# Top-10 cross-attention: reordered input loads and softmax steps in the first two batches

## The reference, cut to what matters

```python
scores = einsum('bnd,d->bn', x, score_w[0]) + score_b[0]      # x: (8, 224, 512)
_, topk_idx = top_k(scores, 10)
sparse = take_along_axis(x, topk_idx)                          # (8, 10, 512)
q = (sparse @ Wq.T + bq), split into 16 heads of 32
k = (ctx @ Wk.T + bk); v = (ctx @ Wv.T + bv)                   # ctx: (8, 750, 512)
attn = softmax(q @ k.T / sqrt(32))
out = x.at[arange(8), topk_idx].set((attn @ v) @ out_w.T + out_b)
```

## Time and profile before

| | |
|---|---|
| median of 3 runs | 141.36 us (141.33 to 141.48) |
| the profiled execution | time 141.29 us, span 139.5 us |
| granted TensorE clock, mean | 0.995 of full speed |
| busy: TensorE, VectorE, ScalarE, GpSimd | 95%, 63%, 18%, 5% |
| moved by DMA | 37.52 MB, mean 269 GB/s |

### The profile page before, as it was taken

The page is one execution under the profiler, slowest core; times in us unless marked ns, Lnnn a source line. Parts: engine busy times, 40 slices in busy tenths (PEclk is TensorE's granted clock), DMA queues, the critical chain, the costliest instruction groups (busy, mean ns, idle before and its releaser), DMA issues.

```text
span 139.5 us, 3090 instructions
## 1 busy us (share of the span) xinstructions
PE 132.1 (95%) x1298; PEld 126.2 (90%) x1298; DVE 88.5 (63%) x247; ACT 24.9 (18%) x53; POOL 7.5 (5%) x34
## 2 busy tenths in 40 slices
PE   4989999899999999999999999999999999999980
PEld 2567999789999999999999999999999999999970
DVE  1798696899890577287870575077218799874150
ACT  4122400030322160003140031004101400231110
POOL 7700000003000000000000000000000000000002
PEclk9999999999999999999999999999999999999998
DMA  4999999999997189999989985996691092000001
GB/s 131 415 414 417 409 411 401 444 434 413 416 385 308 46 332 401 271 401 435 427 328 314 318 343 147 318 324 266 222 316 45 5 331 120 0 0 5 0 5 47
DMA packets 6958, 37.52 MB, mean 269 GB/s; under 512 B 961, under 2 KB 961, under 8 KB 4642
## 3 DMA queue, kind: packets, MB, share of 16 engines
q1 hardware_dynamic: 6528, 37.00, 69.7%
q0 software_dynamic: 128, 0.33, 0.7%
q10 hardware_dynamic: 290, 0.01, 0.2%
HBM read 33.50 MB, written 3.83 MB: 268 GB/s over the span
## 4 chain that ended last, share of the span: by engine, by line
PE 72%; DMA 14%; SPq 7%; issue 2%; DVE 1%; POOLq 1%; POOL 0%; DVEq 0%
PE mix_ps L846 38%; PE logits_ps L827 23%; DMA ctx_r<-ctx_rows_dram 14%; PE logits_ps L813 5%; SPq L205 3%; SPq L212 3%; PE logits_ps L785 2%; PE logits_ps L751 1%; PE mix_ps L785 1%; POOLq L60 1%; DVE o_T L610 1%; PE misc_ps L859 1%; DVE heads L607 1%; PE logits_ps L859 0%; SPq L218 0%
## 5 line engine op out<-in xcount | busy, mean ns | idle before, releaser
L846 PE MATMUL mix_ps<-probs,ctx_r 125*128 125x160 f32 x384 | 54.0, 300 | 0.3
L846 PEld LDWEIGHTS mix_ps<-probs,ctx_r 125*128 125x128 f32 x384 | 52.5, 190 | 0.8 <-DMA ctx_r<-ctx_rows_dram 0.4
L827 PE MATMUL logits_ps<-qk,ctx_c 128*125 128x160 f32 x240 | 33.4, 299 | 0.0
L827 PEld LDWEIGHTS logits_ps<-qk,ctx_c 128*125 128x125 f32 x240 | 32.9, 188 | 0.0
L813 PE MATMUL logits_ps<-qk,ctx_c 128*125 128x160 f32 x144 | 20.6, 302 | 0.7 <-DMA ctx_c<-ctx_cols_dram 0.7
L533 DVE TENSOR_REDUCE col_max<-logits_ps 125x160 f32<-125x960 f32 x8 | 9.3, 1157 | 18.8 <-PE logits_ps L827 15.2
L813 PEld LDWEIGHTS logits_ps<-qk,ctx_c 128*125 128x125 f32 x144 | 19.7, 187 | 1.1 <-DMA ctx_c<-ctx_cols_dram 0.9
L361 ACT ACTIVATE mix<-mix_ps 128x320 f32<-128x320 f32 x16 | 7.0, 439 | 62.1 <-PE mix_ps L846 62.1
L572 DVE TENSOR_REDUCE prob_sum<-probs 125x160 f32<-125x960 f32 x8 | 14.7, 1842 | 4.4 <-ACT probs L357 4.4
L357 ACT ACTIVATE probs<-probs 125x480 f32<-125x480 f32 x16 | 9.3, 603 | 30.3 <-DVE probs L565 30.3
L408 DVE CUSTOM_DVE_ANT_0 product<-x_sb,score_w_sb 112x513 f32<-112x513 f32 x16 | 10.4, 692 | 1.3 <-DMA x_sb<-x_lines_dram 1.2
(11 more groups left out here) (130 smaller groups left out, 96.1 us busy)
## 6 DMA issues: line engine op xcount, KB each, us to landing
ctx_r<-ctx_rows_dram SPq DMA_DIRECT2D x8, 1536.0 KB, 8.0
ctx_c<-ctx_cols_dram SPq DMA_DIRECT2D x6, 1500.0 KB, 10.8
x_sb<-x_lines_dram SPq DMA_DIRECT2D x8, 520.0 KB, 9.5
out_dram<-x_sb SPq DMA_DIRECT2D x8, 448.0 KB, 12.8
ctx_c<-ctx_cols_dram SPq DMA_DIRECT2D x2, 750.0 KB, 14.5
ctx_c<-ctx_cols_dram SPq DMA_DIRECT2D x4, 375.0 KB, 15.5
wq_sb<-wq_dram SPq DMA_DIRECT2D x1, 1024.0 KB, 7.5
wk_sb<-wk_dram SPq DMA_DIRECT2D x1, 1024.0 KB, 10.0
```

The lines of the kernel that those rows point to most:

```text
L827: last = nc.tensor.matmul(logits_ps[n][0:S_P, t // BANK_T, (t % BANK_T) * HQ:(t % BANK_T + 1) * HQ], ctx_c[n][:, f, t, :], qk[:, b, f, :], ...
L846: last = nc.tensor.matmul(mix_ps[half][:, f * HQ:(f + 1) * HQ], ctx_r[n][0:S_P, t, c:c + P], probs[n][:, t, :], start=(t == 0), stop=(t == ...
```

## The change

- SP: the score weights are issued first on SP's queue and no longer by ScalarE. Among the first loads, the columns' parts move ahead of inputs: part 0 of batch 0 ahead of input 4, part 1 ahead of input 5, the first two parts of batch 1 ahead of input 6, the third ahead of input 7. Rows 0 are loaded in two parts, each with its own semaphore (`part_rows_in`).
- SP waits for `gathered` ahead of columns 3.
- VectorE: the maximum is taken in two halves, by PSUM banks, each behind its own semaphore (`first_logits`, `logits_done`), and find_shift's reductions take both halves. score(7) moves behind subtract_max(0, 0). The softmax steps of batch 1 move between choose_eight and choose_rest.
- TensorE: weigh(0) becomes `weigh_by_part`, which does context groups 0 to 2 of all four feature tiles first and 3 to 5 after. transpose_scores moves from matmul 8 to 22 of logits(1), transpose_picked from 14 to 15 and project_queries(1) from 19 to 20 of weigh(1).

```diff
+ROW_PARTS = [(0, BANK_T), (BANK_T, S_T)]
...
-        col_max = sb("col_max", [P, HQ])
-        quad_max = sb("quad_max", [P, QUADS, CB])
+        col_max = sb("col_max", [P, 2, HQ])
+        quad_max = sb("quad_max", [P, QUADS, 2, CB])
...
+            def load_rows_part(k):
+                ts = slice(*ROW_PARTS[k])
+                sp.dma_start(ctx_r[0][:, ts, :], ctx_rows[0, :, ts, :]).then_inc(part_rows_in[k], 16)
...
+            sp.dma_start(score_line[:, :], score_row).then_inc(score_w_in, 16)
             load_x(0, 3)
             sp.dma_start(wq_sb[:, :, :], wq).then_inc(wq_in, 16)
             load_x(3, 4)
             sp.dma_start(wk_sb[:, :, :], wk).then_inc(wk_in, 16)
+            load_cols_part(0, 0)
             load_x(4, 5)
-            load_cols_part(0, 0)
+            load_cols_part(0, 1)
             load_x(5, 6)
-            load_cols_part(0, 1)
             load_cols_part(0, 2)
+            load_cols_part(1, 0)
+            load_cols_part(1, 1)
             load_x(6, 7)
-            load_cols_part(1, 0)
+            load_cols_part(1, 2)
             load_x(7, 8)
-            load_cols_part(1, 1)
-            load_cols_part(1, 2)
-            load_rows(0, 0)
+            load_rows_part(0)
+            load_rows_part(1)
             load_rows(1, 1)
             for b in range(B):
                 sp.wait_ge(x_in[b], 16)
             sp.wait_ge(logits_done, 1)
             load_cols(2, 0)
             sp.wait_ge(logits_done, 2)
+            sp.wait_ge(gathered, 16)
             load_cols(3, 1)
...
-            act.dma_start(score_line[:, :], score_row).then_inc(score_w_in, 16)
...
             def find_max(b, n):
-                dve.wait_ge(logits_done, b + 1)
-                nc.vector.tensor_reduce(col_max[0:S_P, :], tiles(n).rearrange("p k t c -> p c k t"), AX.XY, ALU.max)\
-                    .then_inc(max_step, 1)
+                for k, done in enumerate((first_logits, logits_done)):
+                    dve.wait_ge(done, b + 1)
+                    nc.vector.tensor_reduce(col_max[0:S_P, k, :], tiles(n)[:, k, :, :].rearrange("p t c -> p c t"), AX.X, ALU.max)\
+                        .then_inc(max_step, 1)
...
             score(6)
             find_max(0, 0)
-            score(7)
             find_shift(0)
             subtract_max(0, 0)
+            score(7)
             choose_eight()
-            choose_rest()
-            move_idx()
             find_max(1, 1)
             find_shift(1)
             subtract_max(1, 1)
+            choose_rest()
+            move_idx()
...
+            def weigh_by_part():
+                for k, (t0, t1) in enumerate(ROW_PARTS):
+                    pe.wait_ge(part_rows_in[k], 16)
+                    pe.wait_ge(exp_done, k + 1)
+                    for half in range(2):
+                        for f in range(2):
+                            c = (2 * half + f) * P
+                            for t in range(t0, t1):
+                                last = nc.tensor.matmul(mix_ps[half][:, f * HQ:(f + 1) * HQ], ctx_r[0][0:S_P, t, c:c + P],
+                                                        probs[0][:, t, :], start=(f == 0 and t == 0), stop=(t == S_T - 1),
+                                                        skip_group_check=True)
+                        if k:
+                            last.then_inc(mix_ready[half], 1)
...
-            logits_by_step(1, 1, [], {8: transpose_scores})
-            weigh(0, 0, {})
-            weigh(1, 1, {14: transpose_picked, 19: lambda: project_queries(1)})
+            logits_by_step(1, 1, [], {22: transpose_scores})
+            weigh_by_part()
+            weigh(1, 1, {15: transpose_picked, 20: lambda: project_queries(1)})
```

More of the change, by code:

```diff
@@ L166, in build @@
         ctx_r_in = [sem(f"ctx_r_in{n}") for n in range(2)]
+        part_rows_in = [sem(f"part_rows_in{k}") for k in range(len(ROW_PARTS))]
         consts_cleared, numbers_done, vec_consts = sem("consts_cleared"), sem("numbers_done"), sem("vec_consts")
@@ L181, in build @@
         pair_done, low_copied, high_copied = sem("pair_done"), sem("low_copied"), sem("high_copied")
-        logits_done, max_step, shift_spread, shift_done = sem("logits_done"), sem("max_step"), sem("shift_spread"), sem("shift_done")
+        first_logits, logits_done, max_step, shift_spread, shift_done = sem("first_logits"), sem("logits_done"), sem("max_step"), sem("shift_spread"), sem("shift_done")
         heads_cleared, key_heads_done, key_rows_done = sem("heads_cleared"), sem("key_heads_done"), sem("key_rows_done")
@@ L531, in find_max @@
             def find_max(b, n):
-                dve.wait_ge(logits_done, b + 1)
-                nc.vector.tensor_reduce(col_max[0:S_P, :], tiles(n).rearrange("p k t c -> p c k t"), AX.XY, ALU.max)\
-                    .then_inc(max_step, 1)
+                for k, done in enumerate((first_logits, logits_done)):
+                    dve.wait_ge(done, b + 1)
+                    nc.vector.tensor_reduce(col_max[0:S_P, k, :], tiles(n)[:, k, :, :].rearrange("p t c -> p c t"), AX.X, ALU.max)\
+                        .then_inc(max_step, 1)
             def find_shift(b):
-                at = 8 * b
+                at = 9 * b + 1
                 dve.wait_ge(max_step, at + 1)
-                nc.vector.tensor_reduce(quad_max[:, 0, :], col_max[:, :].rearrange("p (k c) -> p k c", c=QUAD), AX.X, ALU.max,
-                                        apply_transpose=True).then_inc(max_step, 1)
+                nc.vector.tensor_reduce(
+                    quad_max[:, 0, :, :].rearrange("p k c -> p (k c)"),
+                    col_max[:, :, :].rearrange("p k c -> p (k c)").rearrange("p (k c) -> p k c", c=QUAD), AX.X, ALU.max,
+                    apply_transpose=True).then_inc(max_step, 1)
                 dve.wait_ge(max_step, at + 2)
                 for q in range(1, QUADS):
-                    nc.vector.tensor_copy(quad_max[0:QUAD, q, :], quad_max[q * QUAD:(q + 1) * QUAD, 0, :]).then_inc(max_step, 1)
+                    nc.vector.tensor_copy(quad_max[0:QUAD, q, :, :], quad_max[q * QUAD:(q + 1) * QUAD, 0, :, :]).then_inc(max_step, 1)
                 dve.wait_ge(max_step, at + 5)
-                nc.vector.tensor_reduce(all_max[:, :], quad_max[0:QUAD, :, :].rearrange("p q k -> p k q"), AX.X, ALU.max)\
+                nc.vector.tensor_reduce(all_max[:, :], quad_max[0:QUAD, :, :, :].rearrange("p q k c -> p c (q k)"), AX.X, ALU.max)\
                     .then_inc(max_step, 1)
@@ L623, in _ @@
             nc.vector.memset(ones[:, :], 1.0).then_inc(vec_consts, 1)
-            nc.vector.memset(col_max[:, :], LOWEST).then_inc(vec_consts, 1)
+            nc.vector.memset(col_max[:, :, :], LOWEST).then_inc(vec_consts, 1)
             dve.wait_ge(numbers_done, 3)
@@ L816, in logits_by_step @@
                             skip_group_check=True)
+                        if f == DT - 1 and t == BANK_T - 1:
+                            last.then_inc(first_logits, 1)
                 last.then_inc(logits_done, 1)
@@ L829, in logits @@
                             ctx_c[n][:, f, t, :], qk[:, b, f, :], start=(f == 0), stop=(f == DT - 1))
+                    if t == BANK_T - 1:
+                        last.then_inc(first_logits, 1)
                 last.then_inc(logits_done, 1)
+            def weigh_by_part():
[11 more added lines that the diff above has]
+                            last.then_inc(mix_ready[half], 1)
             def weigh(b, n, between):
-                pe.wait_ge(ctx_r_in[n], (b // 2) * 16 + 16)
+                pe.wait_ge(ctx_r_in[n], (b // 2) * 16 + (16 if n else 0))
                 pe.wait_ge(exp_done, 2 * b + 1)
```

## The result

The changed kernel takes 145.97 us (median of 6 runs, 145.31 to 147.33) against 141.42 us for the kernel before: ratio 1.0316, 95% interval 1.0264 to 1.0369. It is slower by 4.5 us; forecast were 3.4. The profiled execution took 145.31 us with a span of 143.6, so it is the shortest of the six, 4.1 us above the span of before. Some executions, of the kernel before too, take 2 to 4 us more than the rest of the same kernel, and the ratios leave them out, so that a median and its ratio can differ slightly.

A forecast was written before the change was run, and what follows sets the result against it. PE, busy without a gap from 51.7 to 130.2 us, was taken as the bound, so delay entering counts: context 4 puts logits(4) 3.4 us late, span 139.5 + 3.4 = 142.9, median 144.8 us, range 143.0 to 146.6.

The forecast's parts named there:

- Input 6: First loads: two column parts now ahead of input 6 land it at 24.4 to 24.5 us instead of 22.1.
- VectorE's steps: First softmax: find_max in halves 1.3 us, find_shift 2.76, subtract_max 1.14, then score(7) 1.23, ending at 32.3.
- The wait at step 22: Logits(1): PE reaches transpose_scores at about 29.5 us and waits 2.9 us for all 16 scores, until 32.35.
- The early chain: Start of the kernel, up to logits(0) at 16.64 us: taken as unchanged, bounds -0.4 and +0.4 us.
- What followed the wait: After transpose_scores: transposes 0.27 us, last two matmuls 0.54, weigh(0) from 33.2 for 6.52, ending at 39.7.
- PE's own delay: TensorE before logits(4): 1.9 us late after transpose_picked, so logits(4) would begin at 73.4 without context 4's delay.
- Weigh(1) and the gather: Weigh(1) begins at 39.7 us; gather issued at 41.5, takes 2.6, lands at 44.1; PE waits 0.4 at step 15.
- Context 4: SP's queue behind the gather: columns of context 4 land at 74.9 us instead of 71.2, delaying logits(4); chance 0.58.
- Sum: Whole kernel: logits(4) 3.4 us late with no PE gap after, so span 142.9 us and median 144.8.
- Front alone: Rival: only the 1.9 us front stall counts, as the queue makes up its idle time: 143.3 us; chance 0.17.
- A gather slow in an empty queue: Rival: the gather stays slow, delaying SP and context 4: 146.7 us at 4.5, 149.8 at 7.6; chance 0.12.
- rows 0 in parts and maximum by banks: Row parts at weigh(0) are worth nothing; bank maximum shortens later softmaxes by some 0.3 us and saves nothing.

The follow-up runs named there:

- the second trace: The changed kernel run once more, unaltered, for another trace: median 146.13 us, ratio 1.0282 to the kernel before; the profiled execution took 147.14 us.
- The run with inputs back: Changed kernel with the loads of inputs 6 and 7 back in their old places among the column parts: 145.84 us, ratio 1.0246.
- the run with two copies late: Changed kernel with two of the five early copies of input moved behind the last load of rows: 144.55 us, ratio 1.0229.
- old-order run: Changed kernel with inputs 4 to 7 in their old places and score weights on ScalarE's queue: 143.18 us, ratio 1.0104.
- the run with ratio 0.9996: Changed kernel with the old order of first loads, score weights on ScalarE's queue and two input copies behind the last rows: 141.53 us.

## Why the prediction was right, point by point

- **Input 6.** Forecast 24.5, used at 25.03. The chain goes through it in both traces of the changed kernel, and with the whole old order weigh(0) is at 31.34 again.
- **VectorE's steps.** Forecast 1.3, 2.76, 1.14 and 1.23; measured 1.26, 2.79, 1.13 and 1.32 to the end of score(7) at 32.87 (32.3 forecast, nearly all of the difference being input 6). Right.
- **The wait at step 22.** Forecast 2.9 us, measured 2.4. PE came there at 30.5, not 29.5 (the forecast's own terms, 23.2 + 22 x 0.272 + 0.4, give 29.6), because logits(0) began 1.1 us late. The early chain, which I took as unchanged within 0.4 us, was 1.1 late in this execution and 0.1 late in the second; in both weigh(0) began at 34.2 to 34.4, so it cost nothing.
- **What followed the wait.** This is the term that was mis-sized most: "the last two matmuls (0.54)" and "33.2 + 6.52 = 39.7". Behind 2.4 us of idle PE they took 0.95 and 7.80 us, at the granted clock shown above, 1.7 us more together. In the second trace they took 1.09 and 8.61. PE's own delay at logits(4) was 75.32 - 0.27 - 71.47 = 3.6 us where I had 1.9. The run with inputs back, where the wait was 0.6 us, had its weigh(0) in 6.52. Not all of the 1.7 is the clock's price: 1.7 us sooner, PE would have come to step 15 at 44.4 and waited for the gather, so the clock added some 0.9 to PE's own delay (an estimate from 46.09 and 45.1).
- **Weigh(1) and the gather.** The gather was issued at 41.92 (41.5) and took 3.2 us (2.6), to 45.1 (44.1). The late gather is the other term that was mis-sized, by 1.0 us. TensorE did not wait for it here, as it was itself late. In the run with two copies late, at full clock, TensorE waited 0.7 for it and was 3.4 us late in the end; in the old-order run it waited 0.7 as well. The estimate from the Trainium skill ("DMA: Bandwidth & Descriptors", "Anatomy of one DMA") was 2.4 us; the traces have 3.1 to 3.8 in an empty queue and 6.4 to 7.6 in a full one, and they decide.
- **Context 4.** Forecast to land at 74.9, landed 75.28. The backlog behind the gather was sized well: context 4 was forecast 30.8 us after the gather, and in the five traces with five early copies and SP's wait it lands 30.2 to 31.4 us after it. The chain leads from context 4 back to its issue and so to weigh(0), but the moment of the issue did not decide: in the first trace the DMA engines have a share of 1.02 from 51 to 80 us, and in all of them the landing does not follow the issue (12.7 us later in the earlier trace rows, 13.2 to 14.5 here). So context 4 hangs on the gather, and the gather on VectorE and input 6. The wait on it was shorter than the 1.5 forecast in the first trace (0.3) because PE came later, near it in the second (1.1). Its share is 1% where PE is not late by itself (old-order run with and without late copies).
- **Sum.** Context 4 ended last, as forecast, and put logits(4) 3.9 us late instead of 3.4: the gather landed 1.0 later, and what followed took 0.6 less. Another 0.27 us lies in logits(4) itself, 6.79 instead of 6.52, as weigh(0) had it behind its own wait in the earlier trace rows. In all eleven traces that were read the span is the start of logits(4) in the timeline plus 68.1 to 68.3 us, so nothing behind it counts, as was said. That the error in PE's own delay did not show is luck: PE was 3.6 us late by itself, and context 4 brought just a little more. With context 4 in time the kernel still takes 144.55 (two copies late), where the forecast's terms for the front alone gave 143.3. The median of 145.97 lies above the 145.31 of the first trace; in the second trace context 4 lands 31.4 us after the gather instead of 30.2, and the gather takes 3.8 us.
- **The rivals.** Front alone: no; removing the load order leaves 1%. A gather slow in an empty queue: no. That nothing was gained by rows 0 in parts and maximum by banks is supported only in sum, by the run with ratio 0.9996; neither was undone by itself.

What stays open: why context 4 lands up to 2 us later in one execution than in another, and whether it ends last in the executions that have no trace. Of the 4.5 us, 1.2 (by the ratios) go away when context 4 alone is in time; the rest is carried by TensorE's own delay as well.

## What to carry to other kernels

When inputs are reordered in a saturated stream, follow each displaced load to the engine that uses it in program order, and look for the next load that decides once the first is repaired. A wait put on a queue cost nothing here where the event was early, and where it was late it held everything behind it; the load with the smallest margin stood some 30 us further on. A stall of TensorE can cost more than its own length: behind the stalls of 2.4 to 3.9 us that were traced the matmuls ran at a lower clock for a while. Whether that counts depends on what comes later: here a load that ended last covered it.

## What the runs showed that I had not expected

- After 2.4 to 3.1 us of waiting for the scores, weigh(0)'s 48 instructions took 7.80, 8.20 and 8.61 us instead of 6.52, at a granted clock down to 0.50. The length of the wait does not set the loss: in the run with context 3 not behind the gather they took 7.1 after 2.9 us. After waits of 0.6 and 0.8 us in the same place they took 6.52.
- Early matmuls can run at about half speed while the clock row says 1.00: picking rows took 1.94 us in the first trace and 1.07 in the second of the same kernel. In the run with two late copies this went on to 20.5 us.
- A gather of 80 rows of 2 KB took 3.1 to 3.8 us with no load beside it, and 6.4 to 7.6 with one.
